# A cross-attention and feed-forward chain on one core: one PSUM copy moved from ScalarE to VectorE in one step out of four, and TensorE's padding at one place, behind a branch

## The reference, cut to what matters

```python
x = x + L0_xattn(layernorm(x), ctx)          # 16 batches of 128 tokens, width 128, 16 heads
x = x + L0_ffn(layernorm(x))                 # six layers: local attention, then a gated feed-forward
x = x + L1_xattn(layernorm(x), ctx)
x = x + L1_ffn(layernorm(x))                 # two layers of the same kind, 8 heads, window 64
# L0_ffn, one layer:
q, k, v = split(shift(x) @ Wqkv)             # 16 heads of 64
q, k = rotate(l2norm(q) * qs), rotate(l2norm(k) * ks)
p = softmax(8 * q @ k.T + mask)              # windows of 32 tokens and the one before
x = (p @ v) @ Wo + x
a, g = split(layernorm(shift(x)) @ W1 + b1)
x = (a * gelu(g)) @ W2 + b2 + x
```

## Time and profile before

| | |
|---|---|
| median of 3 runs | 2202.27 us |
| lowest, highest | 2198.31, 2203.32 us |
| profiled execution, its own time | 2202.99 us |
| profiled execution, span | 2201.2 us |
| TensorE, VectorE, ScalarE, GpSimd busy | 95%, 83%, 76%, 63% of the span |
| granted TensorE clock, mean | 0.985 |

### The profile page before, as it was taken

The page is one execution under the profiler, slowest core; times in us unless marked ns, Lnnn a source line. Parts: engine busy times, 40 slices in busy tenths (PEclk is TensorE's granted clock), DMA queues, the critical chain, the costliest instruction groups (busy, mean ns, idle before and its releaser), DMA issues. The chain is left out here.

```text
span 2201.2 us, 90075 instructions
## 1 busy us (share of the span) xinstructions
PE 2082.7 (95%) x33646; PEld 1433.0 (65%) x33646; DVE 1822.4 (83%) x4873; ACT 1682.5 (76%) x5850; POOL 1390.0 (63%) x1318
## 2 busy tenths in 40 slices
PE   7989999999999999999999999999998887899997
PEld 5656666666666666666666666666666664666665
DVE  5888888888888888888888889888886588888873
ACT  4767888888888888888888888888887335788784
POOL 1337777777776777777676777767674125666660
PEclk9999999999999999999999999999999998999999
DMA  4001222112211222112221122112211100000001
GB/s 117 5 3 36 73 61 50 42 51 68 59 46 43 67 61 52 44 46 74 61 49 44 51 66 61 45 45 56 54 49 39 31 17 6 14 16 11 16 6 29
DMA packets 144806, 97.03 MB, mean 44 GB/s; under 512 B 61977, under 2 KB 137409, under 8 KB 144385
## 3 DMA queue, kind: packets, MB, share of 16 engines
q1 hardware_dynamic: 143232, 91.02, 16.3%
q10 hardware_dynamic: 1152, 0.26, 0.1%
HBM read 23.11 MB, written 1.05 MB: 11 GB/s over the span
## 5 line engine op out<-in xcount | busy, mean ns | idle before, releaser
L739 PE MATMUL bank<-wqkv,hs 128*128 128x512 f32 x1344 | 658.8, 610 | 4.9 <-ACT arena L1595 2.5
L1983 POOL TENSOR_TENSOR arena<-arena,rnorm 128x512 f32<-128x512 f32 x448 | 455.5, 1046 | 281.8 <-DVE rnorm L259 280.6
L1976 POOL TENSOR_TENSOR arena<-arena 128x512 f32<-128x512 f32 x448 | 567.0, 1276 | 57.8 <-DVE arena L2196 57.6
L1624 ACT ACTIVATE arena<-bank,amx 128x64 f32<-128x64 f32 x1536 | 459.0, 337 | 14.3 <-DVE amx L2247 14.1
L1624 ACT ACTIVATION_READ_ACCUMULATOR arena<-bank,amx 128x1 f32 x1536 | 354.0, 230 | 0.0
L739 PEld LDWEIGHTS bank<-wqkv,hs 128*128 128x128 f32 x1344 | 229.8, 191 | 177.9 <-issue 157.7
L2191 DVE TENSOR_TENSOR arena<-bank,rot 128x512 f32<-128x512 f32 x448 | 306.4, 684 | 35.5 <-PE bank L739 33.5
L760 PEld LDWEIGHTS bank<-ident,arena 128*128 128x128 f32 x1792 | 211.5, 141 | 188.2 <-issue 116.9
L2196 DVE TENSOR_TENSOR arena<-bank,rot 128x256 f32<-128x256 f32 x896 | 333.2, 413 | 0.0
L1601 ACT ACTIVATE arena<-bank 128x512 f32<-128x512 f32 x426 | 252.1, 628 | 102.2 <-PE bank L760 102.1
L1990 POOL TENSOR_TENSOR arena<-arena,ainv 128x512 f32<-128x512 f32 x192 | 200.5, 1044 | 195.2 <-DVE ainv L2255 195.2
(11 more groups left out here) (226 smaller groups left out, 3306.2 us busy)
## 6 DMA issues: line engine op xcount, KB each, us to landing
arena<-arena SPq DMA_DIRECT2D x768, 64.0 KB
wqkv<-in_L_ffn_Wqkv_dram SPq DMA_DIRECT2D x24, 256.0 KB
hs<-z SPq DMA_DIRECT2D x128, 32.0 KB, 1.8
hs<-z SPq DMA_DIRECT2D x128, 31.8 KB, 1.9
fx<-z SPq DMA_DIRECT2D x31, 128.0 KB, 2.2
fx<-z SPq DMA_DIRECT2D x31, 127.0 KB, 2.5
wqkv<-in_L_ffn_Wqkv_dram SPq DMA_DIRECT2D x24, 128.0 KB
w<-in_L_ffn_W_dram SPq DMA_DIRECT2D x6, 341.0 KB
```

Of the source, the lines that this page charges most:

```text
L739: nc.tensor.matmul(bank[o][:], src[:], wqkv[w][:, off:off + 512], start=True, stop=True).then_inc(AT[name] if part < 2 else AT[name][i], 1)
L1624: ins = nc.scalar.activation(pb[i][0][p % 2][:, h * DH:(h + 1) * DH], bank[3 + g][:, j * DH:(j + 1) * DH], ACT.Exp, bias=amx[p % 2][:, i, ...
L1976: nc.gpsimd.tensor_tensor(t, t, rs[i][c], ALU.add).then_inc(AT["ak" if c else "aq"][i], 1)
L1983: nc.gpsimd.tensor_tensor(t, t, rnorm[p % 2][:, i, HU * c:HU * c + HU].unsqueeze(2).to_broadcast([P, HU, DH]), ALU.mult).then_inc(AT["mk" ...
```

## The change

Two things. In the Gelu steps the copy of unit 0's turned probabilities out of bank 5 goes from ScalarE to VectorE, which does it behind its copy of the turned keys. And TensorE's align directives of both places in the even steps are gone; in their stead there is one in each odd step from 3 to 95, ahead of `turn(0, s-1, 1)`, with another offset and with `max_nops=0` (47 directives, two of them in phase 0 and phase 2 of every four steps).

```diff
-FETCH_BLOCK, KEYS_AT, OUTPUTS_AT = 256, 62, {0: 254, 2: 251}
+FETCH_BLOCK, SCORES_AT = 256, 60
...
-                    if live(s - 7) and live(s) and s % 2 == 0:
-                        pe.addr_align(FETCH_BLOCK, offset=OUTPUTS_AT[s % 4])
...
-                    if live(s - 3) and live(s - 1) and s % 2 == 0:
-                        pe.addr_align(FETCH_BLOCK, offset=KEYS_AT)
+                    if live(s - 3) and live(s - 1) and s % 2:
+                        pe.addr_align(FETCH_BLOCK, offset=SCORES_AT, max_nops=0)
...
                     if live(s - 2):
-                        probs_all(0, s - 2)
+                        if not (c == 2 and f >= 0 and s < hi):
+                            probs_all(0, s - 2)
                         values(1, s - 2)
...
+                def probs_all(p):
+
+                    dve.wait_ge(AG["pt"][0][0], p + 1)
+                    at(dve, AT["o"][0], p)
+                    nc.vector.tensor_copy(pbt[0][0], bank[5][:]).then_inc(AG["pte"][0][0], 1)
...
                     if s < hi and (s - 7) % 4 == 2 and s >= 7:
                         turned(s - 1)
+                        probs_all(s - 2)
```

## The result

The changed kernel takes 2172.24 us (median of 4 runs, 2169.03 to 2174.98); the kernel before took 2202.33 in the same comparison. The ratio is 0.9863, 95% interval [0.9844, 0.9882]: 30.1 us less. The profiled execution took 2173.06 us.

The account below looks back on a forecast made before the run. TensorE, busy 95% of the span, was taken as the bound, so only its idle time or own work counts. 20.9 + 4.5 + 2.7 + 1.7 = 29.8 us off the median 2202.27 gave 2172 us, range 2163 to 2184.

Parts of the forecast that it names:

- The copy: Gelu steps: without TensorE's wait for ScalarE's copy of bank 5, each gains 0.95 us, 22 times, 20.9 us.
- the wait at the values: Gelu steps: values wait for ScalarE's copy of unit 1's turned keys, giving back 0.33 us of the 1.29.
- ScalarE sets the pace: Gelu steps: TensorE gains only what ScalarE is advanced by, 0.48 us each, 10.6 us; total 2183 us, chance 0.12.
- The hold of phase 1: Ahead of the projection out (L852): "issue" waits, read as an instruction block coming late, go; 4.5 us, up to 5.
- Steps 4 and 6: TensorE's 1.44 and 1.93 us idle behind 47 and 45 NOPs go; 1.7 us counted, bounds 0 and 3.4.
- GpSimd's wait of step 8: A wait of 1.32 us, in a chain through VectorE, expected to take back part of 3.37 us won earlier.
- Step 96: TensorE's idle time for "issue" behind 58 NOPs goes, counted in full at 2.67 us.
- The branch: 47 branches over padding, hidden by some 2.3 us of queued work in odd steps; cost taken as 0.
- refetch: Rival: the branch discards what was fetched ahead and the block comes again; 41 us, total 2213 us, chance 0.07.

Follow-up runs that it names:

- the first experiment: The kernel before with only VectorE's copy of the turned probabilities new and the old NOP padding kept: 2187.77 us, ratio 0.9929.

## Why the prediction was right

**The copy.** Forecast 0.95 us a Gelu step, measured 1.04. The wait vanished, VectorE had the room for it, and what is late next is what the prediction named: values for the turned keys, 0.27 us of idle time. By the distances from one start to the next, over all Gelu steps, the values come 0.337 us later behind the scores, against the 0.33 forecast, and the turn gives back 1.28 us against 1.29. For the wait at the values the prediction allowed 0.14 us behind the end of ScalarE's key copy, with no row for it; in the changed kernel the values start 0.10 us after that end (on the mean, and in each of the 21 Gelu steps from 300 to 1700 us). So the term was 1.9 us too small in the sum, 0.09 us in each of 22 steps. "ScalarE sets the pace" (0.48 a step) is refuted by the first experiment.

**The hold of phase 1.** Forecast 4.5, measured 5.4, the upper bound of 5 slightly passed. The mechanism was inferred from slot counts; branches in place of the NOPs left it (a step of phase 1 at 16.27 us), and moving the block's end by ten slots removed it (16.06 us). Both were needed: the first alone would allow anything about that place. One reading of the prediction was wrong here. It put the crossing before the held one "about 3 us earlier" and read the hold from that closeness. In the trace of the kernel before, with the block's first matmul as the mark, the two are at least 3.64 us apart, and in phase 3 a pair of 3.70 us isn't held. What differs is the packet: it starts 1.1 us after the crossing before it in phase 1 and 0.1 us in phase 3, on the mean. In phase 1 it ends only 1.4 to 1.8 us before the block's first matmul, in phase 3 2.0 to 2.7.

**Steps 4 and 6.** Forecast 1.7 of 3.4, measured 3.8. This is the term that was furthest off. I expected a part to be lost in GpSimd's wait of step 8; that wait rose by 0.2 us only, so VectorE and GpSimd had moved forward with TensorE. It was 3.8 and not 3.4 chiefly because modelled ends hide 0.16 us of each idle stretch, a correction that the prediction made for phase 1 and forgot here.

**Step 96.** The idle time is gone, but what stands behind step 95 varies by 7 us between profiles, so the 2.67 us can't be read from the total.

**The branch.** Zero on the path was right, with 2.0 us of cover measured where I had put 2.3. Its price for the sequencer is 0.17 to 0.38 us in the records by their medians, 0.23 apart in a chain. The twelve branches more make a Gelu step 0.81 us longer. No refetch showed: with the target in the same block (offset 60) and in the next one (offset 36), whose packet had ended at least 3.0 us before its first matmul, no wait for "issue" stands behind a branch between 300 and 1700 us. No run branches further.

**What was not foreseen.** Phase 0 is 0.13 us longer. It is not a hold for a late block: between 300 and 1700 us the changed kernel's blocks had all arrived at least 2.5 us before their first matmul. It is the distance between the two separate waits ahead of the values, which come 19 slots behind a block's end there. They are 0.28 us apart in 16 of 20 steps, where 0.11 us is usual, and TensorE has little left to start at that point: when the first wait's record begins, at 1024.64 us, five matmuls of the scores are still to start, the last 0.09 us later. In the rows of the changed kernel for that step's two pairs (first and last start; the second pair is the one behind the block's end):

```profile
L810 PEldq EVENT_SEMAPHORE  x2: 51/51/51, 1018.8 to 1024.6; - x2
L811 PEldq EVENT_SEMAPHORE  x2: 51/51/51, 1018.9 to 1024.9; - x2
```

With the end elsewhere (offsets 80 and 36) it vanishes. What the sequencer does there I can't tell from the records. With the chain of 13 branches and with NOPs (a phase 0 step of 16.58 and 16.60 us) it vanishes too, at an unchanged offset, and for that I have no explanation.

That the total came within 0.3 us is luck in part: the three terms were 4.9 us too small together and the end behind step 95 was 4.4 us shorter where 2.7 were forecast; against that stand 3.4 us of phases 0 and 3 and a first step that began 3.0 us later in this execution.

## What to carry to other kernels

Where an engine's idle time is "issue", count the slots to the next multiple of a block before explaining it by the program: the hold that kept its slot and changed its matmul here (193 or 194 modulo 256, 40 of 40) was a late block, and moving the block's end by five matmuls removed the one of phase 1 (16.27 to 16.06 us a step). Padding was not free here, though a NOP is recorded with 13 ns: multiply their number by the pitch, 77 ns, and compare with the matmuls queued ahead, some 1.8 to 2.0 us here; a branch, 0.23 us apart in a chain, takes the place of any more than three or four of them. And test two parts of a change apart and together: here a copy was worth 16 us in one layout of the instructions, and with the padding's own 11 us the two together gave 30.

## What the runs showed of the hardware that I had not expected

- In the kernel without a directive a block of 256 slots was never used sooner than 1.2 us after the end of its packet; where TensorE was held, 1.2 to 1.6 us. Packets took 0.9 to 1.8 us over all runs. When a packet starts is not settled: from 0.2 us before the crossing ahead of it to 2.7 us after it in the kernel before, and up to 6.8 us after it in the kernel without a directive (crossings taken at the block's first matmul).
- A branch over padding (taken each time: no NOP is recorded in those runs) stands on TensorE's queue with 170 to 378 ns by its medians (0.23 us apart in a chain; single ones up to 2.02 us), a NOP with 13 ns at 77 ns apart. By 0.23 and 0.077 us one branch weighs as much as three NOPs.
- The layout of the instructions alone, with every matmul in its place, is worth 70 us in 2172 here, 3%.
- In the old layout a gain in one step made the blocks come late in the next: in phase 3 the packet started 1.0 us after the crossing ahead of it on the mean instead of 0.1, and ended 1.2 to 1.7 us before the block's first matmul instead of 2.0 to 2.7. Why it starts later was not tested.
